# A graph network kernel: 72 dense blocks in place of 76, seven gather steps beside each in place of six, deeper count lists for the first nodes

## The reference

```python
agg = segment_sum(x[src], dst);  deg = segment_sum(1, dst)
h = relu(concat([x, agg / max(deg, 1)]) @ W_fc + b_fc) + x @ W_res + b_res
x = layernorm(x + h)
# two general convolutions, with a relu between them, then
conv(x) = segment_sum(x[src] @ Wm + bm + edge_attr @ We + be, dst) + x @ Ws + bs
x = layernorm(x + conv2(relu(conv1(x))))
```

## Time and profile before

| | |
|---|---|
| Runs | 3587.72, 3590.77, 3591.53 us; median 3590.77 |
| Profiled execution | span 3585.2 us, 114,923 instructions |
| TensorE busy | 3167.6 us, 88% |
| VectorE busy | 2339.3 us, 65% |
| ScalarE busy | 1613.7 us, 45% |
| GpSimd busy | 2021.8 us, 56% |
| Indirect gathers of rounds 0 to 2 | 1368, mean 1119 ns |
| HBM over the span | 267 GB/s |

### The profile page before, as it was taken

How to read it: one execution, slowest core, us unless ns; L and a number is a source line. 1 busy time by engine, 2 the same in 40 slices (tenths; PEclk the granted TensorE clock), 3 DMA queues, 4 the chain that set the end, 5 groups by cost and what they waited for, 6 DMA issues and landing times.

```text
span 3585.2 us, 114923 instructions
## 1 busy us (share of the span) xinstructions
PE 3167.6 (88%) x39408; PEld 2958.1 (83%) x39408; DVE 2339.3 (65%) x5369; ACT 1613.7 (45%) x2096; POOL 2021.8 (56%) x2292
## 2 busy tenths in 40 slices
PE   0239999999999999889999889999999889999995
PEld 0127988888888888778888879999999889999995
DVE  8779998888888888779999682333333423333335
ACT  0123677878999999788988650000000400000000
POOL 6761234445666666534444256666666666666664
PEclk9869999999999999999999979999999999999998
DMA  3521455556666666668888429999999599999996
GB/s 92 134 18 70 167 194 198 218 213 233 238 240 251 251 238 240 245 207 247 248 246 247 147 93 400 403 402 402 402 402 403 202 354 403 402 402 402 402 402 241
DMA packets 232872, 959.10 MB, mean 268 GB/s; under 512 B 44815, under 2 KB 144285, under 8 KB 173818
## 3 DMA queue, kind: packets, MB, share of 16 engines
q1 hardware_dynamic: 186027, 884.48, 65.0%
q0 software_dynamic: 46784, 73.84, 6.8%
HBM read 694.75 MB, written 263.40 MB: 267 GB/s over the span
## 4 chain that ended last, share of the span: by engine, by line
PE 68%; DVE 11%; issue 8%; POOL 6%; DVEq 3%; ACT 2%; DMA 2%; SPq 0%; ACTq 0%; POOLq 0%
PE ps L1109 48%; PE ps L1132 10%; DVE union L805 5%; PE ps L1179 4%; PE ps L1101 3%; POOL abuf L1213 3%; DVE union L921 2%; ACT union L1416 1%; DVE abuf L932 1%; POOL union L1213 1%; PE ps L1069 1%; DVEq L466 1%; DVEq L932 1%; PE ps L1188 1%; POOL abuf L1255 0%
## 5 line engine op out<-in xcount | busy, mean ns | idle before, releaser
L1271 POOL DMA_INDIRECT msg<-y_tab,idx x1368 | 1531.1, 1119 | 1041.9 <-ACT idx L1377 652.0
L1109 PE MATMUL ps<-union,abuf 128*128 128x192 bf16 x14896 | 1265.3, 247 | 13.9 <-DVEq L782 10.2
L1109 PEld LDWEIGHTS ps<-union,abuf 128*128 128x128 f16 x14896 | 1226.7, 98 | 21.2 <-issue 10.6
L1398 ACT ACTIVATE abuf<-ps 128x784 f16<-128x784 f32 x1216 | 1000.7, 823 | 239.9 <-PE ps L1132 212.3
L805 DVE TENSOR_TENSOR union<-lane,union 128x1568 f16<-128x1568 f16 (+3 forms) x1440 | 949.5, 710 | 31.0 <-PE ps L1132 27.1
L1109 PE MATMUL ps<-early,abuf 128*128 128x195 bf16 x7546 | 853.4, 249 | 0.0
L1109 PEld LDWEIGHTS ps<-early,abuf 128*128 128x128 f16 x7546 | 677.1, 99 | 100.9
L1132 PE MATMUL ps<-union 128*128 128x392 f16 (+2 forms) x4288 | 689.5, 288 | 52.4 <-DVE union L805 47.1
L1377 ACT ACTIVATE idx<-src_g 128x6 int32 (+1 forms) x228 | 46.4, 205 | 1280.2 <-PE ps L1101 1277.9
L1179 PE MATMUL ps<-union 128*64 128x128 f32 x7280 | 444.4, 278 | 48.2 <-ACT union L1416 48.1
L1179 PEld LDWEIGHTS ps<-union 128*64 128x64 f32 x7280 | 394.1, 137 | 98.4 <-DVE abuf L932 79.2
(11 more groups left out here) (229 smaller groups left out, 1241.4 us busy)
## 6 DMA issues: line engine op xcount, KB each, us to landing
abuf<-a_dram SPq DMA_DIRECT2D x304, 1568.0 KB
a_dram<-abuf SPq DMA_DIRECT2D x76, 3136.0 KB
union<-in_edge_attr_dram SPq DMA_DIRECT2D x728, 160.0 KB, 2.9
msg<-y_tab,idx POOLq DMA_INDIRECT x1368
y_tab<-union SPq DMA_DIRECT2D x28, 336.0 KB, 2.2
abuf<-in_x_dram SPq DMA_DIRECT2D x28, 224.0 KB, 3.4
y_tab<-early SPq DMA_DIRECT2D x7, 682.5 KB, 5.5
out_dram<-union SPq DMA_DIRECT2D x2, 800.0 KB, 3.5
```

What stands on the lines that cost most here:

```text
L1109: last = nc.tensor.matmul(ps[:, bank, 0:3 * width_of[r]], abuf[:, buffer, hi * P:(hi + 1) * P], ycols[r][:, hi, :], start=hi == 0, stop=hi ...
L1271: pool.indirect_dma_start(msg[:, s, 0:3 * width_of[r]], None, y_tab[r], bass.IndirectOffsetOnAxis(ap=idx[:, s:s + 1], axis=0)).then_inc(ga ...
L1398: A.activation(abuf[:, j, :].rearrange("p (h w d) -> p w h d", w=WPB, d=WD) [:, w:w + 2, :, :], ps[:, w % 4:w % 4 + 2, 0:WIN].rearrange("p ...
```

## The change

Three constants, what follows from them, and room for it:

```diff
-FIRST = ((8, 8), (24, 4), (32, 3), (192, 2))
-END = 76
-WITH = 38
+FIRST = ((4, 14), (20, 6), (32, 3), (200, 2))
+END = 72
+WITH = 36
...
         end = REGIONS[n + 1][0] if n + 1 < len(REGIONS) else END
         node = b * P
+        step = -(-step // P) * P
...
-        found.append((b - REGIONS[0][0], end - b, wd, (deeps[0:WPB], deeps[WPB:2 * WPB]), inside[0][4]))
+        found.append((b - REGIONS[0][0], end - b, wd, (deeps[0:WPB], deeps[WPB:2 * WPB]), inside[0][4], before))
+        before += sum(windows * deep for _, _, windows, deep, _ in inside)
...
-    G, GW = 6, 8
+    G, GW = 7, 8
...
-    UNION = max(2 * CW + RINGS, 3 * CW)
+    KEPT = 8 * NB
+    UNION = max(2 * CW + RINGS, 3 * CW, YW + KEPT * D)
...
-        trF = sb("trF", [64, P])[:, :]
+        trF = part_d[0:64, :, :].rearrange("p j d -> p (j d)")[:, 0:P]
...
-                                        dve.wait_ge(stepped, i * pair + (q + s0 + many - HB + 1))
+                                        dve.wait_ge(stepped, i * pair + (q + e0 + many - HB + 1))
```

More of the change, by code:

```diff
@@ L64, in regions @@
 def regions():
-    found, (all_runs, _) = [], runs()
+    found, (all_runs, _), before = [], runs(), 0
     for n, (b, wd, k) in enumerate(REGIONS):
@@ L149, in gnn_program @@
     CW = CG * P
-    spans_of = [(s0, (REG + [(0, 0, 0, 0, CW)])[n + 1][4], wd) for n, (_, _, wd, _, s0) in enumerate(REG)]
+    spans_of = [(s0, (REG + [(0, 0, 0, 0, CW)])[n + 1][4], wd) for n, (_, _, wd, _, s0, _) in enumerate(REG)]
     PIECES = 16
@@ L167, in gnn_program @@
     assert UNION >= YW >= BLOCKS * D and G * F1 <= 512 and 0 < GI <= ITERS and all(b <= 2 * GI or b - n >= 2 * GI for n, b in ((r[1], r[0] + r[1]) for r in REG)) and B0 >= 0 and DB % 2 == 0 and WPB % HB == 0
-    assert all(n % 2 == 0 and s0 % P == 0 and sum(d) * WD // wd % RING == 0 for _, n, wd, ds, s0 in REG for d in ds) and HIS % 2 == 0 and (SETS - SETS % 2) * G >= T + BLOCKS - 1
+    assert all(n % 2 == 0 and s0 % P == 0 and sum(d) * WD // wd % RING == 0 for _, n, wd, ds, s0, _ in REG for d in ds) and HIS % 2 == 0 and (SETS - SETS % 2) * G >= T + BLOCKS - 1
     ctx = ExitStack()
@@ L236, in gnn_program @@
         hot_c = union[:, 2 * CW:2 * CW + RINGS].bitcast(F16).rearrange("p (s c) -> p s c", s=RING)
-        KEPT = 8 * NB
         x1_head = union[:, YW:YW + KEPT * D].rearrange("p (b d) -> p b d", d=D)
@@ L813, in _ @@
                     step(V.memset(ps[:, 7, :], 0.0), "zeros")
-                    for b0, blocks, wd, deeps, s0 in REG:
+                    for b0, blocks, wd, deeps, s0, e0 in REG:
                         upto, pair = steps_upto(wd, deeps)
@@ L1125, in _ @@
                                     if q % many == 0:
-                                        pe.wait_ge(made, i * (pair // HB) + ((q + s0 + many) // HB))
+                                        pe.wait_ge(made, i * (pair // HB) + ((q + e0 + many) // HB))
                                     if c == 0 and w % 2 == 0:
@@ L1396, in _ @@
                                 for w in range(0, WPB, 2):
-                                    act.wait_ge(stepped, i * pair + (upto[j][w + 2] + s0 + AHEAD))
+                                    act.wait_ge(stepped, i * pair + (upto[j][w + 2] + e0 + AHEAD))
                                     A.activation(abuf[:, j, :].rearrange("p (h w d) -> p w h d", w=WPB, d=WD)
@@ L1518, in _ @@
                 if r == 0:
-                    for b0, blocks, _, _, _ in REG:
+                    for b0, blocks, _, _, _, _ in REG:
                         with sp.Fori(0, blocks // 2) as i:
```

## The result

The changed kernel takes 3667.48 us (median of four runs, 3664.27 to 3669.36); the kernel before takes 3589.80 us beside it. The ratio is 1.0214, with a 95% interval of 1.020 to 1.0227. The forecast was 3578 us with a range to 3612, so the sign and the range are both wrong.

The account below looks back on a forecast made before the run. The bound changes: VectorE, then TensorE in round 0; in rounds 1 and 2 GpSimd's gathers would take over from TensorE and DMA. -31.3 + 18.7 = -12.6 us on the median 3590.77 gave 3578 us, range 3518 to 3612.

Parts of the forecast that it names:

- -31.3 + 18.7 = -12.6 us: Whole kernel: round 0 and before it gain 31.3 us, rounds 1 and 2 lose 18.7 us.
- Round 0, -31.3: Round 0 and its preparation: four four-wide blocks less, -57.3 us, less the added costs, -31.3 us in sum.
- the first two blocks: Start of round 0, where VectorE is the bound: 32 more count steps for the first 24 nodes, +8.8 us.
- Two-wide blocks: Round 0, 22 blocks: longer mark and seventh add on VectorE, 0.40 us each, +8.8 us.
- four-wide blocks: Round 0, 42 remaining blocks, TensorE the bound: three more small products, +0.10 us each, +4.2 us.
- GpSimd has room too: Round 0, four-wide blocks: seven gathers make 12.5 us, under the block's 14.4 us.
- Round 1, +10.2: Round 1: GpSimd's gathers set the pace, 669.1 us a round, so it ends 10.2 us later.
- Stretched gathers: Rounds 1 and 2: VectorE's marks hold GpSimd's gathers, 71 stalls of 0.40 us, 28.4 us a round.
- the long gaps: Rounds 1 and 2, GpSimd's queue: 4.5 long gaps of 0.98 us more each, 4.4 us a round.
- Round 2, +7.5: Round 2: same pace set by GpSimd's gathers as in round 1, so it ends 7.5 us later.
- GpSimd keeps up: Rival for rounds 1 and 2, chance 0.30: stall below 0.3 us or 0, total 3521 us, from 3518 to 3564.
- the mark blocks more: Rival for rounds 1 and 2, chance 0.22: gathers lock to VectorE's adds; at 1.0 us a stall, 3663 us.

Follow-up runs that it names:

- the unrolling: Changed kernel with VectorE's edge loop unrolled once in place of seven times (`TURNS = 1`): 3643.41 us, ratio 1.0139.
- the pause before the sixth gather: Changed kernel with 68 skipped, plus one semaphore exchange with ScalarE per turn of two blocks in rounds 1 and 2: 3588.01 us, ratio 0.9979.
- 134 skipped: Changed kernel with 134 never-executed VectorE instructions added ahead of the edge loop: 3665.57 us, ratio 1.0185.
- 68 skipped: Changed kernel with 68 never-executed VectorE instructions added ahead of the edge loop: 3587.24 us, ratio 0.9991.
- 60 skipped: Kernel before, without the change, with 60 never-executed VectorE instructions added ahead of the edge loop: 3672.06 us, ratio 1.0208.
- half of the change: Dense blocks to 73, seven gathers beside blocks 0 to 67, old lists for the first nodes, 107 skipped instructions: 3648.06 us, ratio 1.0136.
- the loop written as five: Changed kernel with 68 skipped and cut marks, GpSimd's 36 turns in rounds 1 and 2 written as five successive loops: 3573.91 us, ratio 0.9945.
- the light run: Changed kernel with 68 skipped, most of the dense product and its loads left out in rounds 1 and 2: 3533.5 us (one run).
- 32 skipped: Changed kernel with 32 never-executed VectorE instructions added ahead of the edge loop: 3682.48 us (one run).
- run 37: No run number: 37 counts gathers over 1.15 us in round 2 of the changed kernel with its edge loop unrolled once, 3643.41 us.
- the cut of the mark: Mark cut into one-tile pieces in rounds 1 and 2: changed kernel with 68 skipped 3561.58 us, ratio 0.9929; kernel before 3590.77 us, ratio 0.9996.

## Why the prediction was wrong, step by step

- **The step that failed is the sum itself**, "-31.3 + 18.7 = -12.6 us". It goes from the end of round 0 to the first gather of round 1 without a term. 66.6 us were lost there in the edge loop, by refetched instructions. Shown by five placements, one of them in both kernels, and by the unrolling. The prediction never asked which loops move in VectorE's program when 60 instructions are put ahead of them.
- **Another 19.9 us behind the edge loop** are a matter of TensorE's clock: granted 0.60 over the first 30 us in the changed kernel and 0.99 before, so mostly at its level of 1.2 GHz in place of 2.4; the fold's products take 40.8 us there in place of 22.1. The refetching does not decide the clock: with the pause before the sixth gather the loop ran at 37.15 us an iteration and the clock behind it was 0.59; with 134 skipped it refetched, and the stretch took 135.3 us, as before. TensorE was busy for 447 of the 500 us ahead of it with that pause and for 446 with the 68 skipped alone, whose clock stayed at 0.98, so its load ahead does not tell either. The refetching may still make it likelier. By the times of the single runs the low clock came in three of four of the kernel before with 60 skipped and in four of five with 134, against two of twelve with 68 skipped and three of seventeen of the kernel before beside it; but half of the change had it in all four and the loop written as five in five of six, without refetching. So part of the 19.9 us may be due to the refetching too. What decides it is open; it moves single executions of these kernels by some 15 to 20 us.
- **Round 0, -31.3.** Measured -27.6 at the memset (-24.1 with 68 skipped). Four blocks at 14.33 hold. The preparation and the first two blocks cost 2.6 and 4.9 us, for 1.5 and 9.3. The 9.3 misread the row at 263.59: an operation there is 784 columns wide, eight steps of 98, so two operations make eight steps, not four, and 32 steps cost 8 x 0.548 = 4.4 us. Two-wide blocks cost +0.27 us for 0.40. The other mis-sized term is that of the four-wide blocks, +0.10 each. Before, they took 14.21 and 14.45 us in turn; now it is 14.42 and 14.92: +0.21 and +0.47, mean +0.34, 14 us for 42 blocks in place of 4.2. In every second block TensorE waits 0.31 us for the gathered tiles, the row at 1020.49; why each block pays 0.21 us in place of 0.10 was not looked into. "GpSimd has room too" compared the seven gathers with the block alone. But ScalarE copies their indices only behind its window copies, at 1005.96, though TensorE had used that half at 992.0; the seven then take 12 us, most of them 1.6 us in place of 0.94, and they must land within the 14.2 us from the copy to the time when the product is due. That VectorE's marks are what stretches them there is likely from rounds 1 and 2, and was not tested in round 0.
- **Round 1, +10.2.** Measured +23.5, and +22.6 with 68 skipped. The mechanism is right: GpSimd sets the pace, its waits for the indices are down to 5.5 us, TensorE waits for the tiles, and the DMA share is 0.97, where about 0.96 was forecast. The sizes: 504 x 1.25 = 630 held (the light run is 644.6, with four gaps and a few stretches). Stretched gathers cost 504.1 - 475.9 = 28 us, as forecast (28.4). The mis-sized term is that of the long gaps, forecast at 4.4 us in sum: each was 5.3 to 5.8 us, some 5.3 more than the usual pause of 0.30, four times: 21 us. Why they grew from 1.28 us is open.
- **Round 2, +7.5.** Measured +1.0: the same gaps, but stretches of only 485.3 - 475.7 = 10 us, since fewer marks met a gather: 45 gathers took over 1.15 us in round 1 of the changed kernel, 14 in round 2. That the phase between them was random was too simple; it seems to settle, in round 2 at a good place, in round 1 at a bad one. It is not fixed to the round: round 1 with 32 skipped has 32 such gathers, and round 2 of the unrolled run 37.
- The rivals: "GpSimd keeps up" did not come, "the mark blocks more" gave a time close to the one measured, 3663, by luck: the marks cost what the forecast said or less. The range's lower end, called the no-stall time, is 3521 by the prediction's own sum, not 3518; nothing hangs on it.

## What to carry to other kernels

A loop's price belongs to where its instructions lie. Before an edit is judged, compare the loops it does not touch: the "instruction" queue's packets inside a loop's stretch, and waits for "issue" at its turn, say at once whether it is refetched; a few skipped instructions ahead of it are the control. And an engine that has just become the bound turns costs to be paid that were free before: the cut of the mark is worth nothing at six gathers a block and 0.7% at seven.

## What the runs showed of the hardware

- VectorE fetches its program in packets of 8192 bytes. A loop of 340 instructions ran without any after its first pass when it started 112 behind a multiple of 128 in the compiled program (the kernel before, and 68 skipped), and took about five packets and 5 to 8 us more per iteration at 44, 50 and 76. By where its packets start it lies over four pieces of 128 instructions in the slow placements, and over three in the fast ones. That the engine keeps three such pieces and the one ahead is inferred from that, not shown.
- A turn more of this VectorE loop costs 0.59 us where nothing is refetched (seven turns of 48 instructions took 40.68 us, one turn of the loop written out seven times 37.16).
- A gather of GpSimd that meets a VectorE mark (two SBUF inputs, 1.09 us) takes up to 1.86 us in place of 0.94; with the mark cut in pieces of 0.28 us the longest is 1.18. It looks as if a gather is held until the VectorE instruction under way ends. The Trainium skill, page SBUF — State Buffer, section Who interferes with whom, infers that descriptor writing is spared by such a tensor_tensor. For these gathers the trace disagrees: they take 504.1 us in round 1 with the whole mark and 475.9 us with only its first seventh.
- GpSimd's gathers have a gap after every 112th at fourteen a turn, which ends about 1 us behind the last landing (5.5 us long, 2.1 with light loads), and after every 108th at twelve a turn, of 1.2 us, or none with light loads. What counts them, and why one drains and the other not, is open.
